# The largest-output pass without GpSimd's split, and masked attention with its bias row in two parts

## The chip, the cores and the metric

One core of one Trainium2 chip runs the kernel. The metric is the device time of one execution in microseconds (us); lower is better.

## The reference

A chain of four residual blocks on x of 16 x 256 x 512, with a context of the same shape, all in f32. `_layernorm` has no learned scale.

```
x = x + L0_xattn(layernorm(x), ctx)     # 16 heads of 64; two softmaxes: 77 text rows, 179 image rows
x = x + L0_ffn(layernorm(x))            # 1536 wide, quantized
x = x + L1_xattn(layernorm(x), ctx, ctx, mask)
x = x + L1_ffn(layernorm(x))            # two layers, 2048 wide, routed LoRA
```

In `L0_ffn` every activation is rounded to 16 bits with a scale from the largest magnitude of the whole tensor:

```
up, gate = act_qdq(x @ Wup.T), act_qdq(x @ Wgate.T)
gate = act_qdq(gate * fixed_qdq_u16(sigmoid(gate)))
o = act_qdq(gate * up);  return o @ Wdown.T
```

In `L1_xattn` queries and keys go through the same two linear maps: `p(t) = (t @ W1.T + b1) @ W2.T + b2`, `softmax(p(q) p(k)^T / sqrt(512) + mask) @ ctx`.

## The kernel before

The program is a row of phases, each with its own tiles (their names carry the phase) and a written order of instructions for each engine; engines meet through semaphores. PE is TensorE, DVE VectorE, ACT ScalarE, POOL GpSimd, SP SyncE, which issues most DMAs. An f32 product of full precision is made of three f32r matmuls over a high and a low part of each operand (`product`, L182; lines L186 to L188); the high part is a rounded copy, the low part the difference.

**The output maximum** (`output_maximum`, tiles `om`, L1430 to L1792) must know the largest magnitude of gate * up before the down projection can quantize it. It runs over 48 pieces n of 128 x 1024. For each, SP loads raw up values (L1509) and, every second piece, stored sigmoids (L1513); ACT scales them to int16 `up` (L1582) and writes the `gate` (L1584), and makes every other sigmoid itself (L1575), which DVE rounds into `sq` (L1647); DVE forms `outp` (L1664), the product `prod` of piece n+2 (L1657), and the piece's maximum (L1668). All of these are on one list for each engine, in the order of n.

Beside it the pass prepares the next attention. Both linear maps of query and key are folded into one 512 x 512 matrix (`gram`, n up to 15), and then the folded keys of the context are made in eight chunks of 512 rows, two context blocks x each. A block is loaded into the single buffer `cin` (L1518), turned by PE into PSUM `ctp` (`turn`, L1737), copied by ACT to `craw` (L1590), and POOL makes the high part (cast, L1697) and the low part (subtract, L1699) in `cT`. PE then makes four key groups `rb[i]` and one bias row `tb` of twelve matmuls each. `keys_due`, `bias_due` and `context_due` say at which piece each of these stands: keys (c, i) at n = 16 + 4c + i, contexts 2 to 15 at n = 15, 17, ... 41; contexts 0 and 1 are at n = 3 and 9. ACT adds the column to the keys (L1599) into one of two `rout` buffers, and SP stores them three pieces later (L1522), the bias rows too (L1527). After the last maximum POOL reduces over the partitions (L1727).

**The down projection** (`down`, tiles `dn`, L1795) follows; POOL only issues additions of finished rows to DRAM there.

**Masked attention** (`masked_attention`, tiles `ma`, L1915 to L2226) goes over 16 blocks b, staggered over steps s from FIRST = -3. DVE makes the statistics of x (L2045, L2050) and `var` (L2055); POOL raises it to the power -1/2 (L2016); DVE makes the shift, minus mean times that (L2061); ACT normalises (L2117); PE turns (L2179); ACT and DVE take the high and low part `xT` (L2124, L2065). Keys are split by ACT (L2130) and POOL (L2020), values by ACT (L2136) and POOL (L2024). PE starts each score tile with the bias row, a matmul of one row `trow` with `ones`, both f32 (L2189), then twelve matmuls of a product; DVE adds the mask and finds the maximum (L2073), ACT the exponentials (L2145), PE turns them and multiplies by the values. `LoraSides` (L2229) loads small matrices for the last phase in the meantime; its 20 loads are issued by POOL. `lora_ffn` (tiles `lf`) is not touched.

`wait_alone` (L108) puts a wait on an instruction of its own, with an increment of a spare semaphore behind it.

## Time and profile before

| | us |
|---|---|
| median of 3 runs | 3605.62 (3603.48 to 3608.56) |
| the profiled execution | 3610.11 |
| its span | 3608.4 |
| PE busy | 3250.0 (90%) |
| DVE busy | 1960.4 (54%) |
| ACT busy | 1554.8 (43%) |
| POOL busy | 841.9 (23%) |
| output pass, piece 0 to the last maximum | some 1961 to 2199 |
| masked attention | from some 2493 |

The four engines work beside each other, so shares do not add up. The mean granted clock of TensorE was 0.959 of full speed. Times of single instructions are us from the start of the span.

### The profile page before, as it was taken

How to read it: one execution, taken by the hardware profiler on the slowest of the kernel's cores; microseconds unless marked ns; L12 is line 12 of the kernel's file. 1: busy time of each engine (PE TensorE's matmuls, PEld its weight loads, DVE VectorE, ACT ScalarE, POOL GpSimd, SP SyncE). 2: the span in 40 equal slices, each digit the busy share in tenths (PEclk: the TensorE clock that was granted, in tenths of full speed). 3: DMA queues.
4: the chain of work that ended last, by engine and by line, in shares of the span. 5: the costliest groups of instructions: out<-in, count | busy, mean ns of one | idle time of the engine just before them, and what ended most of it. 6: DMA issues, size and time to landing. Idle time of an engine off the chain costs nothing. (4 is left out here: it accounts for less than half of the span.)

```text
span 3608.4 us, 51546 instructions
## 1 busy us (share of the span) xinstructions
PE 3250.0 (90%) x17336; PEld 2772.8 (77%) x17336; DVE 1960.4 (54%) x3277; ACT 1554.8 (43%) x2947; POOL 841.9 (23%) x1152
## 2 busy tenths in 40 slices
PE   7999979999999987998996886995968999999998
PEld 6989878888888875886885565884756777877776
DVE  3245467777777763555887996553863222222221
ACT  3222266666666652334776775553642111111110
POOL 0000066666666650000000440001730000000000
PEclk9999999999999998999998898997988999999999
DMA  6577654545455425554666676443642100111000
GB/s 182 146 242 229 206 166 145 149 137 150 135 146 152 135 82 198 185 188 150 225 217 218 193 244 214 164 167 112 219 140 79 50 21 21 36 35 36 30 24 12
DMA packets 362213, 503.42 MB, mean 140 GB/s; under 512 B 48835, under 2 KB 227379, under 8 KB 358081
## 3 DMA queue, kind: packets, MB, share of 16 engines
q1 hardware_dynamic: 359130, 491.16, 43.4%
q0 software_dynamic: 2864, 9.42, 0.7%
q8 instruction: 127, 2.08, 0.2%
q14 instruction: 92, 0.75, 0.1%
HBM read 292.83 MB, written 174.08 MB: 129 GB/s over the span
## 5 line engine op out<-in xcount | busy, mean ns | idle before, releaser
L2506 DVE SCALAR_TENSOR_TENSOR lf_hT<-lf_hb,lf_hT 128x512 fp32r<-128x512 f32 x128 | 88.6, 692 | 618.8 <-ACT lf_hT L2571 617.2
L2571 ACT ACTIVATE lf_hT<-lf_hb 128x512 fp32r<-128x512 f32 x128 | 76.6, 599 | 685.2 <-PE lf_py L188 636.3
L769 POOL TENSOR_TENSOR at_prob<-at_prob,at_rec 128x308 f32<-128x308 f32 (+1 forms) x256 | 261.7, 1045 | 264.0 <-DVE at_rec L811 263.4
L904 ACT ACTIVATE at_prob<-at_sc,at_nm 128x77 f32<-128x77 f32 (+1 forms) x1024 | 293.5, 383 | 41.4 <-DVE at_nm L798 41.4
L798 DVE TENSOR_REDUCE at_nm<-at_sc 128x4 f32<-128x308 f32 (+1 forms) x256 | 164.7, 685 | 171.4 <-PE at_sc L958 171.1
L917 ACT ACTIVATE at_pT<-at_tp 128x1024 fp32r<-128x1024 f32 x128 | 131.6, 1028 | 200.8 <-PE at_tp L968 200.8
L186 PE MATMUL lf_hb<-lf_xT,lf_w 128*128 128x512 f32 x512 | 204.9, 400 | 0.0
L188 PE MATMUL lf_hb<-lf_xT,lf_w 128*128 128x512 f32 x512 | 203.7, 398 | 0.0
L187 PE MATMUL lf_hb<-lf_xT,lf_w 128*128 128x512 f32 x512 | 203.2, 397 | 0.0
L188 PE MATMUL lf_py<-lf_w,lf_hT 128*128 128x512 f32 x512 | 202.6, 396 | 0.0
L186 PE MATMUL lf_py<-lf_w,lf_hT 128*128 128x512 f32 x512 | 202.5, 395 | 0.0
L187 PE MATMUL lf_py<-lf_w,lf_hT 128*128 128x512 f32 x512 | 202.0, 395 | 0.0
L186 PE MATMUL dn_py<-qf_wd,dn_om 128*128 128x512 f32 x384 | 150.8, 393 | 26.7 <-DVE dn_om L1868 26.7
L2446 POOL TENSOR_SCALAR lf_var<-lf_mv 128x1 f32<-128x1 f32 x32 | 7.2, 224 | 718.0 <-DVE lf_mv L2459 718.0
L804 DVE TENSOR_REDUCE at_sums<-at_prob 128x4 f32<-128x308 f32 (+1 forms) x256 | 172.8, 675 | 0.0
L186 PE MATMUL pg_bank<-pg_xs,qg_wg 128*128 128x512 f32 x384 | 153.4, 400 | 20.2 <-DVE pg_xs L1362 20.2
L756 POOL TENSOR_TENSOR at_ks<-at_kr,at_ks 128x512 fp32r<-128x512 f32 x128 | 164.8, 1287 | 14.6 <-ACT at_ks L911 14.6
L815 DVE TENSOR_TENSOR at_pT<-at_tp,at_pT 128x1024 fp32r<-128x1024 f32 x128 | 156.2, 1220 | 21.9 <-ACT at_pT L917 21.8
L186 PE MATMUL pu_bank<-pu_xs,qu_wu 128*128 128x512 f32 x384 | 150.6, 392 | 19.0 <-DVE pu_xs L1362 16.7
L186 PE MATMUL at_vq<-at_xT,xo_Wq 128*128 128x256 f32 x512 | 146.7, 287 | 17.6 <-DMA at_xT<-xn_parts 13.1
L186 PE MATMUL at_vq<-at_pT,at_vs 128*128 128x256 f32 x512 | 156.5, 306 | 0.9 <-DVE at_oT L821 0.8
L958 PE MATMUL at_sc<-at_ks,at_qs 128*128 128x256 f32 x1024 | 147.0, 287 | 7.1 <-DMA at_qs<-at_qst 7.1
(323 smaller groups left out, 9648.4 us busy)
## 6 DMA issues: line engine op xcount, KB each, us to landing
at_kr<-k_rows SPq DMA_DIRECT2D x256, 128.0 KB, 2.8
at_qs<-at_qst SPq DMA_DIRECT2D x512, 64.0 KB, 2.0
raw_gate<-pg_stage SPq DMA_DIRECT2D x96, 256.0 KB, 2.0
pu_rg<-raw_gate SPq DMA_DIRECT2D x96, 256.0 KB
raw_up<-pu_stage SPq DMA_DIRECT2D x96, 256.0 KB, 2.1
om_raw<-raw_up SPq DMA_DIRECT2D x48, 512.0 KB, 4.1
dn_raw<-raw_up SPq DMA_DIRECT2D x48, 512.0 KB, 3.8
xn_parts<-pr_xturned SPq DMA_DIRECT2D x32, 512.0 KB, 4.9
```

What stands on the lines that cost most here:

```text
L186: pe.matmul(out, lh, rh, start=start, stop=False, **kw)
L187: pe.matmul(out, lh, rl, start=False, stop=False, **kw)
L188: return pe.matmul(out, ll, rh, start=False, stop=stop, **kw)
L756: pool.tensor_tensor(ks[:, n % NK, :, 1, :], kr[:, n % NKR], ks[:, n % NK, :, 0, :].bitcast(F32), ALU.subtract).then_inc(k_low, 1)
L769: ins = pool.tensor_tensor(prob[:, i, :, lo:hi], prob[:, i, :, lo:hi], rec[:, z, g, :].unsqueeze(2).broadcast_to([P, 2 * NTE, hi - lo]), A ...
L798: ins = dve.tensor_reduce(nm[:, n % 2, g, :], sc[n % 2][:, :, lo:hi], AX_X, ALU.max, negate=True)
L804: dve.tensor_reduce(sums[:, z, g, :], prob[:, i, :, SEG[g][0]:SEG[g][1]], AX_X, ALU.add).then_inc(sum_done, 1)
L815: dve.tensor_tensor(pT[:, n % 2, 1], tp[:], pT[:, n % 2, 0].bitcast(F32), ALU.subtract).then_inc(pt_done, 1)
L904: ins = act.activation(prob[:, i, m, lo:hi], sc[n % 2][:, m, lo:hi], ACT.Exp, bias=nm[:, n % 2, g, m:m + 1])
L917: act.activation(pT[:, n % 2, 0], tp[:], ACT.Copy).then_inc(pt_hi, 1)
L958: ins = pe.matmul(sc[n % 2][:, h * NTE + m, :], qs[:, n % NQ, h, m * P:(m + 1) * P], ks[:, n % NK, h, part, :], start=part == 0, stop=part ...
L2506: dve.scalar_tensor_tensor(hT[:, i, 1, :], hb[i][:], 0.0, hT[:, i, 0, :].bitcast(F32), ALU.max, ALU.subtract).then_inc(h_done, 1)
```

## The change

In the output pass, ACT writes the high part of a context block straight from PSUM into `cT`, and DVE subtracts from the same PSUM tile to get the low part, one piece later, between `products` and `largest`. `craw`, POOL's casts and its subtracts are gone. Context loads are issued by POOL, key and bias stores by ACT one piece after the keys, and `rout` has four buffers with a semaphore each. The turn of a block waits for the low part of the block before. In the down projection POOL raises one column of ones to the power -1/2 at its start.

In masked attention the bias row is loaded as 16 x 256 (`traw`), split by ACT and DVE into two f32r parts, stored to DRAM and loaded as two rows (`trow`), and `ones` has two rows, so that the bias matmul is one f32r matmul. PE waits for it at block 0 only. DVE makes `minus` (minus the mean) before `var`, and POOL the shift, right behind the power. The 20 small loads are issued by SP.

The core of the diff:

```diff
@@ -1512,20 +1513,6 @@
 
-                def load_context(x):
-                    if x:
-                        sp.wait_ge(c_full, x)
-                    sp.dma_start(cin[:], ctx_in[x * S:(x + 1) * S, :].rearrange("(t p) d -> p t d", p=P)).then_inc(c_ready, 16)
-
-                def store_keys(c, i):
-                    sp.wait_ge(r_out, KD * c + i + 1)
-                    sp.dma_start(keys_d[NB * c:NB * (c + 1), :, i, :].rearrange("b p s -> p b s"), rout[:, i % 2, :].rearrange("p (b s) -> p b s", b=NB)
-                                 ).then_inc(r_stored[i % 2], 16)
-
-                def store_bias(c):
-                    sp.wait_ge(t_out, c + 1)
-                    sp.dma_start(bias_d[c:c + 1, :], trow[:, c % 2, :]).then_inc(t_stored[c % 2], 16)
...
-                        load_context(0)
...
-                    if n == 6:
-                        load_context(1)
-                    if context_due(n + 1):
-                        load_context(context_due(n + 1))
-                    if keys_due(n - 3):
-                        store_keys(*keys_due(n - 3))
-                    if bias_due(n - 3) is not None:
-                        store_bias(bias_due(n - 3))
                     if n == 24:
                         sp.wait_ge(gram_low, KD)
                         load_down((0,), (0, KD))
...
-                    if keys_due(n - 3):
-                        store_keys(*keys_due(n - 3))
-                    if n == N:
-                        sp.wait_ge(t_full, NCH - 1)
-                        load_down((0, 1), (2 * KD, 3 * KD))
-                    if bias_due(n - 3) is not None:
-                        store_bias(bias_due(n - 3))
+                sp.wait_ge(t_full, NCH - 1)
+                load_down((0, 1), (2 * KD, 3 * KD))
...
-                    sp.wait_ge(s, 16 * (KD // 2) * NCH)
+                    sp.wait_ge(s, 16 * NCH)
...
@@ -1584,25 +1556,37 @@
                 def context(x):
+                    c, lo = x // 2, x % 2 * S
                     act.wait_ge(c_full, x + 1)
-                    if x:
-                        act.wait_ge(c_low, x)
-                    act.activation(craw[:], ctp[:], ACT.Copy).then_inc(c_out, 1)
+                    if c >= 2:
+                        act.wait_ge(t_full, c - 1)
+                    if c == 1:
+                        act.wait_ge(gc_full, 1)
...
                     if c == 0 and i == 0:
                         act.wait_ge(gc_out, 2)
                         act.wait_ge(gb_low, 1)
-                    if KD * c + i >= 2:
-                        act.wait_ge(r_stored[i % 2], 16 * (2 * c + i // 2))
-                    act.activation(rout[:, i % 2, :], rb[i][:], ACT.Identity, bias=gcol[:, i:i + 1]).then_inc(r_out, 1)
...
 
                 def key_biases(c):
                     act.wait_ge(t_full, c + 1)
                     if c >= 2:
                         act.wait_ge(t_stored[c % 2], 16 * (c // 2))
                     act.activation(trow[:, c % 2, :], tb[0:1, :], ACT.Identity, bias=bb[0:1, 0:1]).then_inc(t_out, 1)
+
+                def store_keys(c, i):
+                    wait_alone(act, r_out, KD * c + i + 1, spacer)
+                    act.dma_start(keys_d[NB * c:NB * (c + 1), :, i, :].rearrange("b p s -> p b s"), rout[:, i, :].rearrange("p (b s) -> p b s", b=NB)
+                                  ).then_inc(r_stored[i], 16)
+
+                def store_bias(c):
+                    wait_alone(act, t_out, c + 1, spacer)
+                    act.dma_start(bias_d[c:c + 1, :], trow[:, c % 2, :]).then_inc(t_stored[c % 2], 16)
 
...
@@ -1630,13 +1614,19 @@
+                    if keys_due(n - 1):
+                        store_keys(*keys_due(n - 1))
+                    if bias_due(n - 1) is not None:
+                        store_bias(bias_due(n - 1))
                     if bias_due(n) is not None:
                         key_biases(bias_due(n))
                     if keys_due(n):
                         keys(*keys_due(n))
                     if context_due(n):
                         context(context_due(n))
+                store_keys(NCH - 1, KD - 1)
                 key_biases(NCH - 1)
+                store_bias(NCH - 1)
 
...
@@ -1656,6 +1646,11 @@
+                def context_low(x):
+                    c, lo = x // 2, x % 2 * S
+                    dve.wait_ge(c_hi, x + 1)
+                    dve.tensor_tensor(cT[c % 2][:, 1, :, lo:lo + S], ctp[:], cT[c % 2][:, 0, :, lo:lo + S].bitcast(F32), ALU.subtract).then_inc(c_low, 1)
...
@@ -1676,6 +1671,12 @@
                         products(n + 2)
+                    if n == 4:
+                        context_low(0)
+                    if n == 10:
+                        context_low(1)
+                    if context_due(n - 1):
+                        context_low(context_due(n - 1))
                     largest(n)
...
@@ -1687,28 +1688,22 @@
-                def context(x):
-                    c, lo = x // 2, x % 2 * S
-                    pool.wait_ge(c_out, x + 1)
-                    if c >= 2:
-                        pool.wait_ge(t_full, c - 1)
-                    if c == 1:
-                        pool.wait_ge(gc_full, 1)
-                    pool.tensor_copy(cT[c % 2][:, 0, :, lo:lo + S], craw[:]).then_inc(c_hi, 1)
-                    pool.wait_ge(c_hi, x + 1)
-                    pool.tensor_tensor(cT[c % 2][:, 1, :, lo:lo + S], craw[:], cT[c % 2][:, 0, :, lo:lo + S].bitcast(F32), ALU.subtract).then_inc(c_low, 1)
-
+                def load_context(x):
+                    if x:
+                        pool.wait_ge(c_full, x)
+                    pool.dma_start(cin[:], ctx_in[x * S:(x + 1) * S, :].rearrange("(t p) d -> p t d", p=P)).then_inc(c_ready, 16)
+
+                load_context(0)
                 pool.memset(betas, 1.0).then_inc(cleared, 1)
...
+                load_context(1)
...
                 for x in range(2, 2 * NCH):
-                    context(x)
...
@@ -1731,7 +1726,7 @@
                     if x:
-                        pe.wait_ge(c_out, x)
+                        pe.wait_ge(c_low, x)
...
@@ -1823,6 +1820,9 @@
+                pool.memset(one[:], 1.0).then_inc(one_made, 1)
+                pool.wait_ge(one_made, 1)
+                pool.tensor_tensor(one[:], one[:], neghalf[:, 0:1], ALU.pow).then_inc(one_raised, 1)
...
-        trow = ph.sb("trow", [1, B, S])
-        ones = ph.sb("ones", [1, P])
+        traw = ph.sb("traw", [B, S])
+        tsplit = ph.sb("tsplit", [B, 2, S], F32R)
+        trow = ph.sb("trow", [2, B, S], F32R)
+        ones = ph.sb("ones", [2, P], F32R)
...
@@ -1989,12 +1993,16 @@
-            sp.dma_start(trow[:].rearrange("o b s -> o (b s)"), bias_d.rearrange("c n -> (c n)").rearrange("(o n) -> o n", o=1)).then_inc(m_ready, 16)
+            sp.dma_start(traw[:], bias_d.rearrange("c (b s) -> (c b) s", b=NB)).then_inc(traw_ready, 16)
             load_keys(1)
...
+            sp.wait_ge(t_low, 1)
+            sp.dma_start(split_d, tsplit[:].bitcast(F32)).then_inc(t_stored, 16)
             load_keys(2)
             load_x(3)
...
+            sp.dma_start(trow[:].bitcast(F32), split_d.rearrange("b a s -> a b s")).then_inc(t_ready, 16)
             for s in range(LAST + 1):
...
@@ -2004,6 +2012,9 @@
                     load_x(s + 4)
+                for i in (2 * s - 6, 2 * s - 5):
+                    if 0 <= i < sides.LOADS:
+                        sides.load(sp, i)
...
@@ -2014,6 +2025,8 @@
                 pool.tensor_tensor(rstd[:, b % 2], var[:], neghalf[:, 0:NK], ALU.pow).then_inc(rstd_ready, 1)
+                pool.wait_ge(rstd_ready, b + 1)
+                pool.tensor_tensor(shift[:, b % 2], minus[:, b % 2], rstd[:, b % 2], ALU.mult).then_inc(shift_ready, 1)
...
 
-            pool.memset(ones[:], 1.0).then_inc(ones_made, 1)
...
                     dve.wait_ge(rstd_ready, b)
+                dve.tensor_scalar(minus[:, b % 2], mv[:, b % 2, :, 0], -1.0, None, ALU.mult)
                 dve.tensor_scalar(var[:], mv[:, b % 2, :, 1], EPS, None, ALU.add).then_inc(var_ready, 1)
-
-            def offset(b):
-                wait_alone(dve, rstd_ready, b + 1, spacer_d)
-                if b >= 2:
-                    dve.wait_ge(xn_ready, b - 1)
-                dve.scalar_tensor_tensor(shift[:, b % 2], mv[:, b % 2, :, 0], -1.0, rstd[:, b % 2], ALU.mult, ALU.mult).then_inc(shift_ready, 1)
...
@@ -2095,10 +2100,11 @@
                     turned_x(s + 1)
-                if 0 <= s + 2 < B:
-                    offset(s + 2)
                 if 0 <= s + 3 < B:
                     statistics(s + 3)
+                if s == FIRST:
+                    dve.wait_ge(t_high, 1)
+                    dve.tensor_tensor(tsplit[:, 1, :], traw[:], tsplit[:, 0, :].bitcast(F32), ALU.subtract).then_inc(t_low, 1)
...
@@ -2157,6 +2163,9 @@
                     keys_high(s + 2)
+                if s == FIRST + 1:
+                    act.wait_ge(traw_ready, 16)
+                    act.activation(tsplit[:, 0, :], traw[:], ACT.Copy).then_inc(t_high, 1)
...
@@ -2186,6 +2195,9 @@
                     cols = slice(t * P, (t + 1) * P)
+                    if b == 0 and t == 0:
+                        pe.wait_ge(ones_made, 1)
+                        pe.wait_ge(t_ready, 16)
                     pe.matmul(sc[b % 2][:, t, :], ones[:], trow[:, b, :], start=True, stop=False)
...
 
-            pe.wait_ge(ones_made, 1)
```

How the order of ACT's instructions changes in the output pass, at a pair of pieces with keys and a context. Before (`om_up`, `qf_gate` and `om_sig` belong to the pieces):

```order
L1584 ACTIVATE qf_gate<-om_prod,scal 128x1024
L1599 ACTIVATE om_rout<-om_rb,om_gcol 128x512
L1582 ACTIVATE om_up<-om_raw,scal 128x1024
L1584 ACTIVATE qf_gate<-om_prod,scal 128x1024
L1575 ACTIVATE om_sig<-qf_gate,scal 128x1024
L1599 ACTIVATE om_rout<-om_rb,om_gcol 128x512
L1590 ACTIVATE om_craw<-om_ctp 128x1024
L1582 ACTIVATE om_up<-om_raw,scal 128x1024
```

and after:

```order
L1556 ACTIVATE qf_gate<-om_prod,scal 128x1024
L1574 ACTIVATE om_rout<-om_rb,om_gcol 128x512
L1554 ACTIVATE om_up<-om_raw,scal 128x1024
L1556 ACTIVATE qf_gate<-om_prod,scal 128x1024
L1547 ACTIVATE om_sig<-qf_gate,scal 128x1024
L1584 DMA folded_keys<-om_rout 128x2x256
L1574 ACTIVATE om_rout<-om_rb,om_gcol 128x512
L1565 ACTIVATE qf_wd<-om_ctp 128x4x256
L1554 ACTIVATE om_up<-om_raw,scal 128x1024
L1556 ACTIVATE qf_gate<-om_prod,scal 128x1024
```

Each key store now stands on ACT, one piece behind its activation, and the context goes to `qf_wd`, where `cT` lies.

The end of POOL's down projection and the start of its masked attention, in order. Before, at the first power (the row `ISA` is an instruction that loads code for POOL):

```order
L2026 MEMSET ma_ones 1x128
L2016 ISA
L2016 TENSOR_TENSOR ma_rstd<-ma_var,neghalf 128x2
L2020 TENSOR_TENSOR ma_rT<-ma_rraw,ma_rT 128x1024
L2016 TENSOR_TENSOR ma_rstd<-ma_var,neghalf 128x2
```

and after, where the down projection starts (the first three rows) and where masked attention does:

```order
L1823 MEMSET dn_one 128x1
L1825 ISA
L1825 TENSOR_TENSOR dn_one<-dn_one,neghalf 128x1
...
L2039 MEMSET ma_ones 2x128
L2027 TENSOR_TENSOR ma_rstd<-ma_var,neghalf 128x2
L2029 TENSOR_TENSOR ma_shift<-ma_minus,ma_rstd 128x2
L2033 TENSOR_TENSOR ma_rT<-ma_rraw,ma_rT 128x1024
```

The `ISA` row of the power's line has moved to the start of the down projection, and the shift follows each power on POOL.

## Rows read from the trace of the kernel before

**Rows 1.** Windows: stretch, us, busy PE, PEld, DVE, ACT, POOL, clock, DMA share, GB/s.

```profile
1976.30:2047.70 71.40, 54.37 (x207) 34.88 (x208) 70.33 (x57) 53.58 (x60) 28.71 (x19) 0.81 0.58 178
2047.70:2197.10 149.40, 123.67 (x531) 98.44 (x529) 139.37 (x107) 114.37 (x126) 55.22 (x26) 0.91 0.76 240
2493.00:2502.00 9.00, 0.00 (x0) 0.00 (x0) 1.71 (x5) 1.06 (x1) 0.00 (x0) 0.50 0.90 320
2560.80:2637.90 77.10, 77.10 (x467) 63.15 (x466) 72.59 (x136) 53.97 (x90) 57.66 (x42) 1.00 0.76 245
```

**Rows 2.** Groups by line, 1960 to 2201 us: busy, mean ns, idle before.

```profile
L1657 DVE TENSOR_TENSOR om_prod<-qf_gate,om_sq 128x1024 f32<-128x1024 int16 x48 | 81.7, 1702 | 18.1 <-DMA om_sq<-gate_sigmoids 17.9
...
L1699 POOL TENSOR_TENSOR qf_wd<-om_craw,qf_wd 128x1024 fp32r<-128x1024 f32 x16 | 48.3, 3021 | 10.1 <-issue 8.9
```

**Rows 3.** Timeline of DVE, output pass: start us, duration us, line, instruction.

```profile
2047.75 1.21 DVE L1664 TENSOR_TENSOR om_outp<-qf_gate,om_up 128x1024 f32<-128x1024 int16 x1
...
2183.26 1.23 DVE L1664 TENSOR_TENSOR om_outp<-qf_gate,om_up 128x1024 f32<-128x1024 int16 x1
...
2190.88 1.23 DVE L1664 TENSOR_TENSOR om_outp<-qf_gate,om_up 128x1024 f32<-128x1024 int16 x1
```

**Rows 4.** Timeline of POOL and DVE in the output pass.

```profile
2163.79 3.25 POOL L1699 TENSOR_TENSOR qf_wd<-om_craw,qf_wd 128x1024 fp32r<-128x1024 f32 x1
...
2164.71 3.41 DVE L1657 TENSOR_TENSOR om_prod<-qf_gate,om_sq 128x1024 f32<-128x1024 int16 x1
```

**Rows 5.** Timeline of all engines, start of masked attention.

```profile
2495.45 0.40 SPq L1992 DMA_DIRECT2D ma_trow<-key_biases  x1
...
2498.67 0.17 DVE L2055 TENSOR_SCALAR ma_var<-ma_mv 128x2 f32<-128x2 f32 x1
2510.04 0.73 POOL L2016 TENSOR_TENSOR ma_rstd<-ma_var,neghalf 128x2 f32<-128x2 f32 x1 [17.05 <-issue]
...
2510.92 2.18 DVE L2061 SCALAR_TENSOR_TENSOR ma_shift<-ma_mv,ma_rstd 128x2 f32<-128x2 f32 x1 [12.09 <-POOL ma_rstd L2016]
...
2524.87 1.22 PE L2189 MATMUL ma_sc<-ma_trow,ma_ones 1*128 1x256 f32 x2
```

**Rows 6.** Costliest groups of the page.

```profile
L815 DVE TENSOR_TENSOR at_pT<-at_tp,at_pT 128x1024 fp32r<-128x1024 f32 x128 | 156.2, 1220 | 21.9 <-ACT at_pT L917 21.8
```

**Rows 7.** Timeline of SP's DMA queue in the output pass.

```profile
2164.04 0.44 SPq L1522 DMA_DIRECT2D folded_keys<-om_rout  x1
```

**Rows 8.** DMA issues, 1961 to 2201 us: KB each, median us to landing.

```profile
om_cin<-in_ctx_dram SPq DMA_DIRECT2D x16, 512.0 KB, 5.3
```

**Rows 9.** Timeline of PE in masked attention.

```profile
2599.97 0.69 PE L2189 MATMUL ma_sc<-ma_trow,ma_ones 1*128 1x256 f32 x2
...
2600.81 0.28 PE L187 MATMUL ma_sc<-ma_rT,ma_xT 128*128 128x256 f32 x1
2600.93 0.27 PE L188 MATMUL ma_sc<-ma_rT,ma_xT 128*128 128x256 f32 x1
...
2608.57 0.69 PE L2189 MATMUL ma_sc<-ma_trow,ma_ones 1*128 1x256 f32 x2
...
2651.61 0.69 PE L2189 MATMUL ma_sc<-ma_trow,ma_ones 1*128 1x256 f32 x2
...
2659.34 0.69 PE L2189 MATMUL ma_sc<-ma_trow,ma_ones 1*128 1x256 f32 x2
```

**Rows 10.** Timeline of DVE and POOL in masked attention.

```profile
2531.15 4.05 DVE L2055 TENSOR_SCALAR ma_var<-ma_mv 128x2 f32<-128x2 f32 x1
...
2602.12 2.38 POOL L2020 TENSOR_TENSOR ma_rT<-ma_rraw,ma_rT 128x1024 fp32r<-128x1024 f32 x1 [2.11 <-ACT ma_rT L2130]
2604.46 2.40 POOL L2024 TENSOR_TENSOR ma_val<-ma_cin,ma_val 128x1024 fp32r<-128x1024 f32 x1
...
2602.27 2.25 DVE L2061 SCALAR_TENSOR_TENSOR ma_shift<-ma_mv,ma_rstd 128x2 f32<-128x2 f32 x1
...
2606.25 0.64 DVE L2055 TENSOR_SCALAR ma_var<-ma_mv 128x2 f32<-128x2 f32 x1
```

More of the change, by code:

```diff
@@ L1930, in masked_attention @@
         rstd = ph.sb("rstd", [P, 2, NK])
+        minus = ph.sb("minus", [P, 2, NK])
         shift = ph.sb("shift", [P, 2, NK])
@@ L2035, in _ @@
                     sides.clear(pool)
-                for i in range(2 * s - 2, 2 * s):
-                    if 0 <= i < sides.LOADS:
-                        sides.load(pool, i)
         @block.vector
@@ L2258, with load @@
     LOADS = 2 * (1 + E) + 2 * 5
-    def load(self, pool, i):
+    def load(self, sp, i):
         layer, i = i % 2, i // 2
```

49 lines of the change are left out of this document (28 added, 21 removed).

## The prediction

> **What bounds the kernel now.** I read the windows view first, for the engines' busy time in four stretches that the change touches [rows 1]. In the output-maximum pass (`om`), pieces 0 to 15 take 71.40 us with VectorE (DVE) busy for 70.33 of them, and pieces 16 to 47, beside which the eight key chunks run, 149.40 us with DVE busy for 139.37, ScalarE (ACT) for 114.37 and TensorE (PE) for 123.67 at a granted clock of 0.91. DVE is what ends last. In the steady steps of masked attention (`ma`) PE is busy for 77.10 of 77.10 us. The fourth stretch, 2493 to 2502, has no matmul at all: it is the start of `ma`.
>
> Second, the groups by line say why DVE is so busy: `prod` has a mean of 1702 ns over 48, and GpSimd's (POOL's) subtract at L1699 of 3021 ns over 16 [rows 2]. Third, DVE's timeline: a pair of pieces without POOL beside it, from `outp` at 2183.26 to `outp` at 2190.88, takes 7.62 us; but 27 pieces lie between the `outp` of piece 16 (2047.75) and of piece 43 (2183.26), so 135.5/13.5 = 10.04 us for a pair [rows 3]. In the difference stands the POOL pair: `prod` is issued at 2164.71 while the subtract runs (2163.79 for 3.25 us) and takes 3.41 us instead of 1.22 [rows 4]. It ends 1.08 us after the subtract, that is, it did not begin before POOL had ended.
>
> Fourth, the start of `ma` [rows 5]: `var` is there at 2498.84, the power that needs it runs at 2510.04, with "17.05 <-issue" of idle before it on POOL: nothing that the profile shows was waited for. The shift, issued when the power is done, is held by POOL's first subtract and ends at 2513.10. ACT's first normalisation and all of PE stand behind it.
>
> **The change, part by part.**
>
> *Output pass, pieces 16 to 47.* Out go POOL's 16 casts and 16 subtracts, and with them what DVE lost to them. In comes a DVE subtract per context, from PSUM and one SBUF tile, 128x1024. No such instruction runs in this pass; the nearest row is attention's L815, the same form and size, mean 1220 [rows 6]. So DVE needs 7.62 + 1.2 = 8.8 us for a pair. ACT needs its busy time of now, 114.37/149.40 x 10.04 = 7.69 us, and now issues two key stores and, every second pair, a bias store. Such a store takes SP's queue 0.44 us [rows 7]; its price on ACT no row shows. With SP's, ACT comes to 7.69 + 2 x 0.44 + 0.1 = 8.7 us; from below it costs nothing (7.7), from above twice the row (9.6), should ACT drain before an issue and fill again behind it. PE needs 123.67/149.40 x 10.04 = 8.3 us. Three engines within 0.5 us that wait for each other don't run at the longest one's own time: I take 9.05, between DVE's 8.8 and ACT's upper 9.6 and nearer DVE's, since that one rests on rows of DVE itself. Gain: 13.5 x (10.04 - 9.05) = **13.4 us** (ends: 13.5 x 0.44 = 6 with ACT at 9.6; 13.5 x 1.24 = 17 with DVE at 8.8).
>
> *Pieces 0 to 15.* Three contexts lie here. Each lost DVE some 2.2 us on one operation (3.41 - 1.22 [rows 4]) and now costs 1.2; the second also about 0.8 by its cast. Gain 3 x 1.0 + 0.8 = **3.8 us** (ends 0 and 6).
>
> *Queues.* SP loses 56 issues, which hid behind its wait for ACT; nothing. Context loads now sit on POOL's queue, which has nothing else left to do but the fold; they wait for the turn before, as on SP. There is one `cin` buffer: issue and landing must fit between one turn and the next. A pair of 9.05 less a turn of about 1.0 less some 0.8 of issue leaves 7.2 us, the median load took 5.3 [rows 8]. Nothing, if POOL's loads land like SP's. The four key buffers free ACT's keys from the store before; ACT was not last, so nothing more. The store one piece later has a full chunk before its buffer comes round. At the pass's end the last piece's maximum still decides; `key_biases` and its store end in the next few us, as today.
>
> *Down projection.* One memset and one power on a single column on POOL, which waits for its first result there: nothing. It makes the code load fall here: the order of instructions has POOL's "ISA" row (the load) now in front of this power, and none left in `ma`.
>
> *Start of `ma`.* With the code there, power (0.73 [rows 5]) and shift follow `var`: 2498.84 + 0.73 + about 0.7 = 2500.3, against 2513.10. But ACT now waits for `traw` ahead of its first normalisation. That load is issued where `trow` is now, 2495.45, behind 2.25 MB; at 320 GB/s [rows 1] those take 7.0 us from 2493, so it lands at 2500 to 2503 (my estimate from these rows); with ACT's copy, 2502.2. Gain **10.9 us** (ends 7, if it lands at 2506, and 12.8). DVE waits in the same place, with the statistics of block 1 behind it, which are wanted 8 us later. PE's new wait for `trow`: split store issued at 2502.7, landing and load 4 us each behind 1 MB of keys and x, so 2511; PE would want it at 2524.87 - 10.9 - 1.6 = 2512.4. Nothing, narrowly; up to 3 us if late.
>
> The Trainium skill ("GPSIMD Engine Reference", section Instruction dispatch) says that the first call of a freshly loaded kernel waits about 6 us for its code, with no instruction in the profile. The row has the same shape but 11.2 us; by the page's figure the term would be some 6 and the sum -31.
>
> *Ramp of `ma`.* Up to block 3 the chain runs through the shift that is held by POOL's subtract, 1.6 us per block: two blocks, **3.3 us** (ends 0 and 5). PE's bias product: f32 pairs of 0.62 us each at full clock (two of its four records: 0.69 [rows 9]) become one f32r pass, 2600.81 to 2600.93, 0.12 [rows 9]: 2 x 0.5 = 1.0 us per block. It counts where PE is last: one block at half clock, where the pair is 1.22 [rows 5] in place of some 0.25, two of them **2.0 us**, and the last blocks, 2651.61 to 2659.34 = 7.73 us each [rows 9], two and a half of them, **2.5 us** (ends for both 2 and 6).
>
> *Steady steps.* PE's 8.60 us (2599.97 to 2608.57 [rows 9]) would become 7.6. But the next limit is there already [rows 10]: POOL's two subtracts, 2602.12 to 2606.86, begin when ACT has cast the keys, and DVE's `var` (issued 2606.25, usually 0.17) ends only at 2606.89; behind it logits, exponentials, ACT's next `xT`. Without the held shift DVE comes to `minus` and `var` at 2604.1, inside the first subtract. If they are let in only when both are over, `var` ends at 2606.95 and the loop remains 8.6 to 8.7: **+0.5 us** over ten steps. For this speaks the `var` at 2531.15, which took 4.05 us, over the end of a subtract and four memsets, back to back [rows 10]. ACT no longer waits for the shift; it waits for the maximum instead.
>
> Side loads go from POOL to SP (about 0.5 us each, two a step); SP has time.
>
> Sum: 13.4 + 3.8 + 10.9 + 3.3 + 2.0 + 2.5 - 0.5 = 35.4 us off. Against the profiled execution's 3610.11 that is 3574.7; the median of the runs shown is 4.5 us lower, 3605.62, so I say **3570 us**.
>
> **Rivals.**
>
> *A, the lock opens between two subtracts.* At 2604.46 the held shift did get in, between POOL's first and second subtract (it ended 2604.52) [rows 10]. If the two `tensor_scalar` do too, `var` is there 2.2 us sooner and the steps fall to PE's 7.6: ten more us, 3560. For it: that row. Against: the row at 2531.15, and that these two are another kind of operation.
>
> *B, the output pass is bound by ACT.* An issue on ACT costs 0.9 us or so and the pair stays at 9.6 to 9.8: 3 to 6 us instead of 13.4, 3579 (3575 to 3584). For it: ACT's 8.7 is already 0.1 under DVE's. Against: SP's 0.44.
>
> *C, slower: the context loads come late.* If POOL's loads land more than 7.2 us after issue, PE's turn waits, the chunk slips, and the waits of ACT and DVE in order of program pass it to every piece. Each us beyond costs 14; the gains of 35 are eaten at 7.2 + 2.5 = 9.7 us, and at 10.5 it would be 3617. Against: POOL has nothing to compute then. Chance 0.04.
>
> The Trainium skill ("SBUF — State Buffer", section Who interferes with whom) has descriptors of a POOL-issued DMA starve while DVE is in its two-port modes; no run so far shows such a load. By it the load would wait for the `tensor_scalar` that each pair has, which is no more than 0.7 us, and C would still need another 2.
>
> *D, the early power doesn't keep the code.* The load returns before `ma`; the 10.9 go, 3581. Against: no other POOL code is called between, by the order of instructions.
>
> **How the numbers follow.** Forecast 0.54, A 0.18, B 0.18, D 0.06, C 0.04. The low end is A with the output term at its upper end (3560 - 4, less a little for the ramp's: 3554); the high end is B or D with traw late or the ramp term missing (3581 + 4, and up to 7 for both together: 3592). A run tells apart about 0.2%, 7 us. Faster by more: all but C and the tail of B and D together, 0.93; within: 0.03; slower: 0.04.
>
> **What would show it.** In `om`: `prod` with a mean near 1.22 us, the new subtract at 1.2, pairs of 9.0 us; POOL without busy time there; ACT's gap behind an issue 0.4 (right) or 0.9 (B); PE waiting for `om_cin` (C). In `ma`: the power within 1 us of `var`, ACT's first normalisation at 10 to 11 us earlier against `var`, its release the `traw` load; bias rows of PE at 0.12; steady period 8.6 with `var` ending where POOL's second subtract does (right) or 7.6 (A). It is wrong if the pair is over 9.6 or under 8.7, or if the first normalisation still stands 14 us behind `var`.

## The result, and the profile after

| | before | changed |
|---|---|---|
| median, us | 3606.10 (4 runs, 3603.48 to 3608.56) | 3578.22 (4 runs, 3576.30 to 3586.45) |
| ratio | | 0.992, 95% interval 0.9905 to 0.9935 |
| profiled execution, us | 3610.11 | 3577.34 |
| span, us | 3608.4 | 3575.7 |
| POOL busy, us | 841.9 | 777.6 |

The kernel became faster by 27.9 us. Forecast were 35 (3570), range 3554 to 3592. The sum came out well by luck: two of its parts were wrong in opposite ways. The output pass gave less than said, masked attention more.

The windows view of the changed kernel, core 0; the stretches are pieces 0 to 15, pieces 16 to 47, and steady masked attention:

```profile
core 0: us, PE busy (x) PEld busy (x) DVE busy (x) ACT busy (x) POOL busy (x), PEclk, DMA share, GB/s
1978.70:2047.00 68.30, 47.45 (x160) 28.84 (x161) 66.02 (x59) 50.74 (x57) 18.45 (x15) 0.73 0.55 167
2047.00:2195.10 148.10, 129.47 (x577) 103.77 (x575) 132.21 (x122) 116.38 (x129) 8.69 (x12) 0.95 0.79 255
2532.00:2619.50 87.50, 87.50 (x550) 75.03 (x550) 63.62 (x160) 65.84 (x110) 60.93 (x42) 1.00 0.81 252
```

Against [rows 1], pieces 0 to 15 went from 71.4 to 68.3 us, the rest from 149.4 only to 148.1, though POOL, which held DVE up before, is busy for 8.69 us instead of 55.22. DVE is busy for 132.21 us of it now and waits for the rest. Pair for pair, from the `outp` of piece 16 (2047.01) to that of piece 43 (2179.90): 132.9/13.5 = 9.84 us, where [rows 3] gave 10.04.

DVE's groups in the output pass, in the view of [rows 2] (busy, mean ns, idle before):

```profile
L1647 DVE TENSOR_TENSOR om_prod<-qf_gate,om_sq 128x1024 f32<-128x1024 int16 x48 | 60.4, 1259 | 23.0 <-DMA om_sq<-gate_sigmoids 23.0
L1652 DVE TENSOR_TENSOR qf_wd<-om_ctp,qf_wd 128x1024 fp32r<-128x1024 f32 x16 | 19.5, 1216 | 0.0
```

`prod` fell from 1702 to 1259 ns, and the new subtract takes 1216. So DVE's `prod` no longer stands behind a subtract of POOL's, and the new instruction costs what was said. But DVE waits now. The view of waits, 2050 to 2180 us (in total, times, longest), for the change:

```profile
ACT qf_wd L1565 <- PE om_ctp L1732: 21.2, 11, 3.6
PE om_ctp L1732 <- DVE qf_wd L1652: 15.8, 8, 4.0
DVE om_prod L1647 <- DMA om_sq<-gate_sigmoids: 13.4, 8, 3.3
```

and for before:

```profile
DVE om_prod L1657 <- DMA om_sq<-gate_sigmoids: 7.6, 4, 2.9
```

In before the view has no wait of ACT for a turn. ACT waited 16.9 us there, nine times, for the key stores that read its two `rout` buffers; with four buffers the change has none of that.

One round of this in the timeline of the changed kernel, which is to be read downwards as a chain:

```profile
2099.80 1.22 DVE L1652 TENSOR_TENSOR qf_wd<-om_ctp,qf_wd 128x1024 fp32r<-128x1024 f32 x1
...
2103.16 1.03 PE L1732 MATMUL om_ctp<-ident,om_cin 128*128 128x128 f32 x8
...
2104.23 1.03 ACT L1565 ACTIVATE qf_wd<-om_ctp 128x1024 fp32r<-128x1024 f32 x1 [2.04 <-PE om_ctp L1732]
2104.42 0.37 ACTq L1584 DMA_DIRECT2D folded_keys<-om_rout  x1
2105.15 1.14 ACT L1554 ACTIVATE om_up<-om_raw,scal 128x1024 int16<-128x1024 f32 x1
...
2106.32 3.54 SPq L1510 DMA_DIRECT2D om_raw<-raw_up  x2
...
2108.37 1.13 ACT L1554 ACTIVATE om_up<-om_raw,scal 128x1024 int16<-128x1024 f32 x1
...
2109.90 0.44 SPq L1514 DMA_DIRECT2D om_sq<-gate_sigmoids  x1
...
2115.08 1.23 DVE L1647 TENSOR_TENSOR om_prod<-qf_gate,om_sq 128x1024 f32<-128x1024 int16 x1 [0.82 <-DMA om_sq<-gate_sigmoids]
```

DVE's low part ends at 2101.02; until then PE may not turn the next block into the one `ctp`. In this round the bias row's matmuls on PE end later still, and it is they that hold the turn to 2103.16; over the 130 us, the waits above give PE 15.8 us for the low part. ACT comes to the context early, waits 2.04 us for the turn, and all its later work is late with it: `up` at 2105.15, the next one at 2108.37. SP's raw loads wait for them (the two issues last from 2106.32 to 2109.86, as the second waits for the second `up`, done at 2109.50), the sigmoid load stands behind them in SP's queue (2109.90), and DVE waits for it till 2115.08. The row 2104.42 is a key store issued on ACT: it lies within the context's copy, and from that copy to the next activation it is 0.92 us.

The start of masked attention, to be set against [rows 5]:

```profile
2495.19 0.16 DVE L2066 TENSOR_SCALAR ma_var<-ma_mv 128x2 f32<-128x2 f32 x1
2495.54 0.73 POOL L2027 TENSOR_TENSOR ma_rstd<-ma_var,neghalf 128x2 f32<-128x2 f32 x1 [6.06 <-DVE ma_var L2066]
2496.35 0.20 POOL L2029 TENSOR_TENSOR ma_shift<-ma_minus,ma_rstd 128x2 f32<-128x2 f32 x1
...
2498.34 0.42 ACT L2168 ACTIVATE ma_tsplit<-ma_traw 16x256 fp32r<-16x256 f32 x1 [2.72 <-DMA ma_traw<-key_biases]
2498.66 1.50 ACT L2123 ACTIVATE ma_xn<-ma_y,ma_shift,ma_rstd 128x512 f32<-128x512 f32 x2
```

The power starts 0.35 us after `var` does (11.37 before), and the shift takes 0.20 behind it. The first normalisation is at 3.5 us behind `var` (14.6 before). What it waits for is `traw`, as predicted, landed at 2498.34, 6.4 us after its issue at 2491.95.

A steady step, against [rows 9, 10]:

```profile
2589.83 2.40 POOL L2033 TENSOR_TENSOR ma_rT<-ma_rraw,ma_rT 128x1024 fp32r<-128x1024 f32 x1 [2.27 <-ACT ma_rT L2136]
2592.19 2.41 POOL L2037 TENSOR_TENSOR ma_val<-ma_cin,ma_val 128x1024 fp32r<-128x1024 f32 x1
...
2591.80 0.46 DVE L2065 TENSOR_SCALAR ma_minus<-ma_mv 128x2 f32<-128x2 f32 x1
2592.17 0.16 DVE L2066 TENSOR_SCALAR ma_var<-ma_mv 128x2 f32<-128x2 f32 x1
...
2595.64 0.38 PE L2201 MATMUL ma_sc<-ma_trow,ma_ones 2*128 2x256 f32 x1
2595.95 0.39 PE L187 MATMUL ma_sc<-ma_rT,ma_xT 128*128 128x256 f32 x1
...
2595.75 1.03 ACT L2130 ACTIVATE ma_xT<-ma_xtp 128x1024 fp32r<-128x1024 f32 x1 [1.61 <-PE ma_xtp L2188]
...
2603.72 1.03 ACT L2130 ACTIVATE ma_xT<-ma_xtp 128x1024 fp32r<-128x1024 f32 x1 [1.61 <-PE ma_xtp L2188]
```

The period is 7.97 us (8.60 before), and PE is busy for 87.50 of 87.50 us. `minus` was issued at 2591.80, inside POOL's first subtract, and ended at 2592.26, when that one was over and POOL's second one had begun. The bias row takes 0.31 us from its start to the next matmul, not 0.12. By the windows above TensorE's granted clock in these steps is 1.00, its upper level (2.4 GHz), as in [rows 1].

### Where the time went

The profiled executions differ ahead of the output pass by several us where the instructions are the same: its first `outp` is at 1976.31 in before, at 1978.73 in the change, and between 1969.85 and 1983.48 in the kernels below. So the table has the time from the first `outp` of the pass to the end of the span (**the rest**). It is 1632.1 us before (one trace) and 1597.0 in the change, 35.1 less; a second trace of the change gave 1596.9. The medians, which contain what lies ahead, moved by 27.9; no row of the changed code accounts for the other 7 us. Two traces of the changed kernel itself differ by 4.8 us ahead of the pass. The gain of the whole kernel is the 27.9.

| stretch | before | changed | difference | forecast |
|---|---|---|---|---|
| pieces 0 to 15 (1976.31 to 2047.75; 1978.73 to 2047.01) | 71.4 | 68.3 | -3.2 | -3.8 |
| pieces 16 to 43 (to 2183.26; 2179.90) | 135.5 | 132.9 | -2.6 | -13.4 |
| from there to `var` of block 0 (2498.67; 2495.19) | 315.4 | 315.3 | -0.1 | 0 |
| `var` of block 0 to its first normalisation | 14.6 | 3.5 | -11.1 | -10.9 |
| `xT` of block 0 to block 4 (2516.87 to 2557.02; 2502.22 to 2532.01) | 40.2 | 29.8 | -10.4 | -5.3 |
| `xT` of block 4 to block 15 (to 2651.71; 2619.65) | 94.7 | 87.6 | -7.1 | +0.5 |
| behind it | 956.7 | 956.1 | -0.6 | -2.5 |

From the first normalisation to the first `xT` both kernels take 3.6 us. How far traces of the same code differ can be read from the kernels below: pieces 16 to 43 took 134.3 to 135.5 us in the three traces with the old output pass, and 132.3 to 133.0 in five with that of the change (the change, c0, b1, b2, b3; a2 is an exception). So the 2.6 us are 1.2 to 3.2, whichever traces are paired, and far from 13.4 in any case.

### The profile page after: what moved, and what is told of

Same layout as the page of the kernel before. It is cut to its first block and busy times, and to the rows that moved or that the text cites. A ratio compares the mean times of both kernels' runs of the same rounds, so it can differ in the third digit from the quotient of the medians.

```text
span 3575.7 us, 51505 instructions
## 1 busy us (share of the span) xinstructions
PE 3239.0 (91%) x17304; PEld 2769.6 (77%) x17304; DVE 1912.3 (53%) x3294; ACT 1553.6 (43%) x2948; POOL 777.6 (22%) x1136
## 5 line engine op out<-in xcount | busy, mean ns | idle before, releaser
L187 PE MATMUL pg_bank<-pg_xs,qg_wg 128*128 128x512 f32 x384 | 153.5, 400 | 20.4 <-DVE pg_xs L1363 20.4
L187 PE MATMUL at_vq<-at_xT,xo_Wq 128*128 128x256 f32 x512 | 147.2, 288 | 19.7 <-DMA at_xT<-xn_parts 12.7
```

The source lines that it names most:

```text
L187: pe.matmul(out, lh, rh, start=start, stop=False, **kw)
```

## The experiments

Medians are set against those of before that were measured beside them, and the rest against the 1597.0 of the change or the 1632.1 of before.

| kernel | median | before there | ratio, 95% | rest | a pair, pieces 16 to 43 |
|---|---|---|---|---|---|
| the change again (c0) | 3577.76 | 3606.70 | 0.991 (0.9895 to 0.9925) | 1596.9 | 9.85 |
| a1 masked attention and power only | 3582.96 | 3609.12 | 0.9929 (0.9907 to 0.9951) | 1601.2 | 10.01 |
| a2 output pass only | 3603.70 | 3609.12 | 0.9982 (0.9971 to 0.9992) | 1622.8 | 9.63 |
| a5 low part early | 3568.09 | 3609.12 | 0.9886 (0.9864 to 0.9907) | 1585.2 | 8.96 |
| a4 sigmoid load first | 3562.72 | 3609.12 | 0.987 (0.9847 to 0.9893) | 1584.3 | 8.90 |
| b4 both | 3558.80 | 3608.12 | 0.9865 (0.9848 to 0.9881) | 1583.5 | 8.92 |
| b1 no early power | 3584.28 | 3608.12 | 0.993 (0.9914 to 0.9947) | 1607.2 | 9.85 |
| b2 bias row in f32 | 3585.23 | 3608.12 | 0.9935 (0.9918 to 0.9953) | 1604.0 | 9.82 |
| b3 shift on DVE | 3589.67 | 3608.12 | 0.9949 (0.9931 to 0.9967) | 1608.1 | 9.80 |
| a3 early power only | 3597.23 | 3606.70 | 0.9969 (0.9955 to 0.9982) | 1621.3 | 9.95 |
| c1 stores on SP | 3583.14 | 3606.70 | 0.9925 (0.9908 to 0.9941) | 1602.5 | 9.99 |
| c2 context loads on SP | 3643.48 | 3606.70 | 1.0099 (1.0083 to 1.0115) | 1665.8 | 14.67 |

c0 is the changed kernel itself, with no edit, measured beside a3, c1 and c2:

> The changed kernel once more, beside the three below on the same chip, as their reference. 26 to 30 us under before.

28.9 us under before, its rest within 0.1 us of the first trace's.

### The two halves apart (a1, a2)

a1 is the changed kernel with the function `output_maximum` of before, of which this is the heart:

```diff
-                    act.activation(cT[c % 2][:, 0, :, lo:lo + S], ctp[:], ACT.Copy).then_inc(c_hi, 1)
+                    act.activation(craw[:], ctp[:], ACT.Copy).then_inc(c_out, 1)
...
-                        pe.wait_ge(c_low, x)
+                        pe.wait_ge(c_out, x)
```

Expected:

> The changed kernel with the output pass of before, so only the early power and the new masked attention are in. Theory 1 (from the two traces: the pass gave 3.5 us, masked attention 29): 29 us under before, about 3577. Rival (the prediction's split: pass 17, attention 18): 18 under before, about 3588.

26.2 us under before, and the rest 30.9 less. The prediction's 18 for this half is out.

a2 is before with the changed `output_maximum`:

```diff
-                    act.activation(craw[:], ctp[:], ACT.Copy).then_inc(c_out, 1)
+                    act.activation(cT[c % 2][:, 0, :, lo:lo + S], ctp[:], ACT.Copy).then_inc(c_hi, 1)
...
-                        pe.wait_ge(c_out, x)
+                        pe.wait_ge(c_low, x)
```

Expected:

> Before with only the output pass of the change. Theory 1: 3 to 4 us under before, 3602.5, which a timing cannot tell from nothing; DVE waits some 13 us for its sigmoid loads, ACT some 20 us for PE's turn. Rival (the pass is worth 17, and masked attention paid it back): 3589.

5.4 us under before, the rest 9.3 less, of which 5.5 in pieces 16 to 43. That is more than the 3.5 read from the two traces, though nearer to it than to 17, and its 130.0 us there stand outside the 132.3 to 133.0 of the same pass in the other traces. The halves add up to 31.6 by medians (27.9 together) and to 40.2 by the rest (35.1 together): the pass alone was somewhat quicker ahead of the old masked attention, with DVE's wait for the sigmoids at 10.0 us instead of 13.4. Why it was is open.

### The ring through `ctp` (a5, a4, b4)

a5 moves DVE's low part ahead of the piece's output:

```diff
                     if n % 2 == 0 and n + 2 < N:
                         rounded(n + 2)
+                    if n == 4:
+                        context_low(0)
+                    if n == 10:
+                        context_low(1)
+                    if context_due(n - 1):
+                        context_low(context_due(n - 1))
                     outputs(n)
                     if n + 2 < N:
                         products(n + 2)
```

Its six lines behind `products` are gone. Expected:

> The changed kernel with DVE's low part of a context placed ahead of the piece's output, two operations (2.3 us) earlier; everything else is as in the change. Theory ring (PE's turn waits for the low part, ACT for the turn, the scaled up values and with them SP's loads are late, and DVE waits for the sigmoids): ACT's wait for the turn falls from 21 us to under 6, DVE's wait for the sigmoids from 13 to under 4, the pair falls from 9.84 towards 8.9, 10 to 12 us under the change, about 3567. Rival memory (the loads are late because the DMA traffic of a faster pass is too dense): ACT's wait goes, the sigmoid wait stays, the time stays within 3 us of the change.

Waits of a5, 2050 to 2180 us:

```profile
ACT qf_wd L1565 <- PE om_ctp L1732: 8.3, 11, 1.3
DVE om_prod L1647 <- DMA om_sq<-gate_sigmoids: 3.1, 2, 2.4
```

ACT's wait for the turn fell from 21.2 to 8.3 us, DVE's for the sigmoids from 13.4 to 3.1, the pair to 8.96 us, the rest by 11.8. The theory said all four, though it had ACT's wait under 6. The rival "the memory is too dense" is out: the same bytes in less time, and the wait went.

a4 leaves the low part where the change has it, and cuts the chain at SP:

```diff
                 def load_main(n):
-                    if n >= 2:
-                        sp.wait_ge(up_ready, n - 1)
-                    sp.dma_start(raw[...]).then_inc(raw_ready[n % 2], 16)
                     if n % 2:
                         if n >= 2:
                             sp.wait_ge(prod_done, n - 1)
                         sp.dma_start(sq[:, 1, :], ...).then_inc(sq_ready, 16)
+                    if n >= 2:
+                        sp.wait_ge(up_ready, n - 1)
+                    sp.dma_start(raw[...]).then_inc(raw_ready[n % 2], 16)
```

> The changed kernel with SP issuing the sigmoid load of an odd piece ahead of that piece's raw load (it stands behind it in the change, and so behind the wait for ACT's up values). Theory ring: DVE's wait for the sigmoids falls from 13 us to under 6, ACT's wait for the turn stays, 5 to 9 us under the change, about 3571. Rival memory: the wait stays at 10 or more and the time within 3 us of the change.

```profile
ACT qf_wd L1565 <- PE om_ctp L1732: 15.1, 13, 2.0
DVE om_prod L1647 <- DMA om_sq<-gate_sigmoids: 1.5, 1, 1.5
```

ACT still waits for the turn (15.1 us, 6 less than in the change), but DVE for the sigmoids only 1.5, and the pair is 8.90 us. So the wait for the turn costs by what stands behind it: with the sigmoid load in time, DVE has next to no gap. The gain, 12.7 us of the rest, is over the 5 to 9 expected.

b4 has both edits:

> The changed kernel with both edits of the output pass: the sigmoid load ahead of the raw load, and DVE's low part ahead of the output. Theory ring: the two cut the same ring at two places, so they don't add up (15 and 10 us alone): DVE is then busy all the time at 8.8 us a pair, 16 to 19 us under the change. Rival (two separate losses): 23 or more.

13.5 us of the rest, the pair at 8.92: hardly more than either alone (12.7 and 11.8), since DVE's own 8.8 is nearly reached; DVE is busy for 130.35 of 135.60 us. The median is 49.3 us under the before measured beside it, where c0 was 28.9 under its own, so 20.4 by the medians. The 16 to 19 expected lie between the two; that the pair is no shorter than in a4 speaks against two separate losses. It is the lowest median tried, 0.9865 (0.9848 to 0.9881), but neither a4 nor a5 can be told from it by the intervals.

### The queues (c1, c2)

c1 gives the key and bias stores back to SP, in the places of before, with the four buffers kept:

```diff
-                    wait_alone(act, r_out, KD * c + i + 1, spacer)
-                    act.dma_start(keys_d[...], rout[:, i, :]...).then_inc(r_stored[i], 16)
+                    sp.wait_ge(r_out, KD * c + i + 1)
+                    sp.dma_start(keys_d[...], rout[:, i, :]...).then_inc(r_stored[i], 16)
```

> The changed kernel with key and bias stores issued by SP three pieces after the keys, as before, four buffers kept. Theory from the trace (an issue on ACT lies within its activations and costs it nothing, 1.04 us from start to start across one; on SP it stands in the queue of the sigmoid loads that DVE waits for): 0 to 4 us over the change, DVE's wait for the sigmoids from 13 to 13 to 18 us. The prediction's term (0.44 us of ACT for each issue, 1 us a pair): ACT gains 13 us and the pass up to that, 3 or more under the change.

Waits of c1, 2050 to 2170 us:

```profile
ACT qf_wd L1584 <- PE om_ctp L1736: 24.8, 11, 3.1
DVE om_prod L1651 <- DMA om_sq<-gate_sigmoids: 14.8, 10, 2.6
```

and two rows of its ACT:

```profile
2103.48 1.03 ACT L1584 ACTIVATE qf_wd<-om_ctp 128x1024 fp32r<-128x1024 f32 x1 [2.04 <-PE om_ctp L1736]
2104.40 1.14 ACT L1573 ACTIVATE om_up<-om_raw,scal 128x1024 int16<-128x1024 f32 x1
```

5.4 us over c0 by the medians, a little over the 0 to 4 expected and with intervals that overlap; 5.5 by the rest, the pair 9.99. From the context's copy to the next activation it is 0.92 us, with no issue between, exactly as in the change with one. So the prediction's 0.44 us of ACT for each issue is out: it is nothing. DVE waits for sigmoids 14.8 us in a stretch of 120 where the change has 12.1. That this is what the move to ACT was worth fits, but is not shown alone: the stores also went back from one piece behind the keys to three.

c2 gives the context loads back to SP, where before has them:

```diff
+                    if context_due(n + 1):
+                        load_context(context_due(n + 1))
```

on SP (with contexts 0 and 1 at n = 0 and 6), and none on POOL. Expected:

> The changed kernel with the context loads issued by SP where before has them. Theory: SP waits for PE's turn with the raw and sigmoid loads behind it, and that turn is now late because of the low part; DVE's wait for the sigmoids rises, 3 to 10 us over the change. Rival C (a load issued by POOL comes later than one of SP's): the turn comes sooner and the time is 2 or more under the change.

66 us over c0, and slower than before. The direction was expected, the size was not. Waits, 2050 to 2170 us:

```profile
DVE om_prod L1657 <- DMA om_sq<-gate_sigmoids: 52.6, 8, 8.8
...
PE om_ctp L1733 <- DVE qf_wd L1662: 44.5, 8, 8.7
...
SPq L1519 <- PE om_ctp L1733: 103.2, 8, 14.6
```

and SP's queue in the timeline:

```profile
2108.54 0.38 SPq L1519 DMA_DIRECT2D om_cin<-in_ctx_dram  x1
2108.96 0.47 SPq L1510 DMA_DIRECT2D om_raw<-raw_up  x1
2109.47 0.68 SPq L1514 DMA_DIRECT2D om_sq<-gate_sigmoids  x1
...
2123.57 0.38 SPq L1519 DMA_DIRECT2D om_cin<-in_ctx_dram  x1
```

SP waits 103 of 120 us for the turn, because its load may only go once `cin` is read; raw and sigmoid loads stand behind it. The turn waits for the low part, the low part stands on DVE behind a `prod` that waits for just those sigmoids (issued at 2109.47, `prod` at 2115.10, the low part at 2120.24). The ring is closed through the lists of three engines, SP, DVE and PE, and one round of it, 15.03 us from 2108.54 to 2123.57, is a pair. In before the same load was at the same place on SP, but the turn waited for ACT's copy only. So of the edits in the pass one (the turn that waits for the low part) needs another (the load off SP's list).

### Masked attention, part by part (b1, a3, b2, b3)

b1 is the change without the memset and the power in `down`:

```diff
-                pool.memset(one[:], 1.0).then_inc(one_made, 1)
-                pool.wait_ge(one_made, 1)
-                pool.tensor_tensor(one[:], one[:], neghalf[:, 0:1], ALU.pow).then_inc(one_raised, 1)
```

> The changed kernel without the one-column power at the start of the down projection. Theory (the early power is what moves the code load): the 11 us between var and the first power of masked attention are back, less the wait for the bias row that now lies beside them (the first normalisation of the change begins 3.5 us behind var): 8 to 9 us over the change, so about 17 under before. Rival (the load is cheap here, or hidden by the wait for the bias row): within 3 us of the change.

```profile
2501.92 0.16 DVE L2061 TENSOR_SCALAR ma_var<-ma_mv 128x2 f32<-128x2 f32 x1
...
2512.78 0.73 POOL L2022 TENSOR_TENSOR ma_rstd<-ma_var,neghalf 128x2 f32<-128x2 f32 x1 [16.69 <-issue]
...
2513.91 1.52 ACT L2118 ACTIVATE ma_xn<-ma_y,ma_shift,ma_rstd 128x512 f32<-128x512 f32 x2 [7.81 <-POOL ma_shift L2024]
```

The load is back in its old place: 10.86 us from `var` to the power, with nothing waited for. The first normalisation stands 12.0 us behind `var`, 8.5 more than in the change, as expected. The rest is 10.2 us longer; the median is 23.8 us under the before beside it, where c0 is 28.9 under, so the medians give 5.1 (ratios 0.993 and 0.991, with intervals that overlap), and not the 8 to 9 expected.

a3 is before with these three lines and nothing else:

```diff
+                pool.memset(one[:], 1.0).then_inc(one_made, 1)
+                pool.wait_ge(one_made, 1)
+                pool.tensor_tensor(one[:], one[:], neghalf[:, 0:1], ALU.pow).then_inc(one_raised, 1)
```

> Before with nothing but the one-column power at the start of the down projection. Theory: the first power of masked attention follows var within 0.5 us instead of 11.2, the shift is then held 2.3 us by POOL's first subtract, and everything behind it comes 10 to 11 us sooner; steady period 8.6 as before: 10 us under before. Rival (the first blocks wait for their loads anyway, which are issued at the same time as before): under 5 us.

```profile
2498.93 0.73 POOL L2021 TENSOR_TENSOR ma_rstd<-ma_var,neghalf 128x2 f32<-128x2 f32 x1 [6.04 <-DVE ma_var L2060]
2499.82 2.17 DVE L2066 SCALAR_TENSOR_TENSOR ma_shift<-ma_mv,ma_rstd 128x2 f32<-128x2 f32 x1 [1.07 <-POOL ma_rstd L2021]
...
2502.12 1.52 ACT L2122 ACTIVATE ma_xn<-ma_y,ma_shift,ma_rstd 128x512 f32<-128x512 f32 x2 [3.03 <-DVE ma_shift L2066]
```

9.5 us under before, 10.8 by the rest. The power follows `var` by 0.35 us, and the shift on DVE is held by POOL's first subtract for 2.17 us, as the prediction said of before. So two instructions on one column are a third of the whole change. Rival D is out by this and by b1.

b2 has the bias row as one f32 row again, loaded straight from `key_biases`, without the split and its waits:

```diff
-        trow = ph.sb("trow", [2, B, S], F32R)
-        ones = ph.sb("ones", [2, P], F32R)
+        trow = ph.sb("trow", [1, B, S])
+        ones = ph.sb("ones", [1, P])
```

> The changed kernel with the bias row as before: one f32 row, an f32 matmul, no split, no round trip through DRAM. Theory (the steps are PE's, and the f32r row takes 0.64 us off each): the steady period is 8.6 us again, 10 steps x 0.64 and some 3 us of the ramp back, less 2 us at the start where ACT waits for the row: 6 to 8 us over the change. Rival (the steps were set by the ring through the shift and POOL's subtracts, and it is the shift on POOL that opened them): period 8.0, within 3 us.

```profile
2560.00:2620.00 60.00, 60.00 (x364) 49.20 (x363) 44.13 (x105) 41.20 (x71) 38.97 (x29) 1.00 0.81 250
```

PE is busy for all 60 us again, and the period is 8.61 us. The rest is 7.0 us longer, within the 6 to 8 expected.

b3 has the shift on DVE, behind `turned_x`, and no `minus`:

```diff
-                pool.tensor_tensor(shift[:, b % 2], minus[:, b % 2], rstd[:, b % 2], ALU.mult)...
+                dve.scalar_tensor_tensor(shift[:, b % 2], mv[:, b % 2, :, 0], -1.0, rstd[:, b % 2], ALU.mult, ALU.mult)...
```

> The changed kernel with the shift made by DVE behind the power as before, and no minus. Theory (two limits stood at the same height, PE's 8.6 and the ring through the shift that POOL's subtract holds): the period stays at 8.5 to 8.6 though PE has 0.64 us less to do, PE shows gaps, 6 to 10 us over the change. Rival (PE alone set it): period 8.0, and only the ramp's 3 us come back.

```profile
2546.10:2622.80 76.70, 74.31 (x458) 61.61 (x457) 73.21 (x136) 53.26 (x93) 48.91 (x27) 1.00 0.83 246
```

```profile
2590.91 2.27 DVE L2068 SCALAR_TENSOR_TENSOR ma_shift<-ma_mv,ma_rstd 128x2 f32<-128x2 f32 x1
...
2594.92 0.61 DVE L2062 TENSOR_SCALAR ma_var<-ma_mv 128x2 f32<-128x2 f32 x1
...
2590.76 2.40 POOL L2030 TENSOR_TENSOR ma_rT<-ma_rraw,ma_rT 128x1024 fp32r<-128x1024 f32 x1 [2.87 <-ACT ma_rT L2140]
2593.12 2.38 POOL L2034 TENSOR_TENSOR ma_val<-ma_cin,ma_val 128x1024 fp32r<-128x1024 f32 x1
```

and of the waits, 2546.1 to 2622.8 us:

```profile
ACT ma_xn L2127 <- DVE ma_shift L2068: 15.0, 9, 1.7
```

The period is 8.52 us (nine steps, 2546.15 to 2622.79), and PE now has gaps: 74.31 of 76.70. The shift is held through POOL's first subtract, ACT's normalisation waits for it in each of the nine steps, and `var`, issued at 2594.92, is held through the end of the second (2595.50). The rest is 11.1 us longer, just over the 6 to 10 expected. So there were two limits, PE at 8.60 and the ring through the shift at 8.52, and either edit alone gives 0.1 us at most of the 0.64 that both give.

## Why the prediction was right in sum and wrong in parts

- **Pieces 16 on: wrong (13.4 forecast, 2.6 came to piece 43).** The gain is under the lower end of 6 us, and the pair, at 9.84, was over the 9.6 that the prediction itself gave as a sign of being wrong. DVE's own 8.8 us a pair was right; a4, b4 and a5 run at 8.90 to 8.96. The step that failed is the one that costs the queues: "they wait for the turn before, as on SP. [...] Nothing". The changed wait of the turn, `c_low` for `c_out`, was named nowhere in the sum. It puts DVE's low part and a turn between ACT's two contexts, and what stands behind ACT's wait (`up`, then SP's raw load, then the sigmoid load) is what DVE waits for. Taking 9.05 because "Three engines within 0.5 us that wait for each other don't run at the longest one's own time" was a margin of 0.25 us in place of a chain that the code shows; it was 1.04.
- **ACT's issue: wrong.** 0.44 us each were forecast; with and without an issue it is 0.92 us from the context's copy to the next activation. Rival B came near the outcome for the pass (9.6 to 9.8, where 9.84 came), with the wrong cause.
- **Pieces 0 to 15: right** (3.8 forecast, 3.2 came).
- **Context loads on POOL: right as far as it went.** They landed in 5.1 us at the median (5.3 on SP), so rival C did not come, neither did the starving of descriptors of which the Trainium skill speaks ("SBUF — State Buffer", section Who interferes with whom) at a size that shows here. But the step saw only a risk in the move; c2 shows 66 us in its favour, as long as the turn waits for the low part.
- **The early power and the start: right** (10.9 forecast, 11.1 came; `traw` released the first normalisation, at 6.4 us after its issue). The price of the load is the row's 11, not the 6 of the Trainium skill's "GPSIMD Engine Reference", section Instruction dispatch.
- **Ramp: half right.** The shift's 1.6 us per block was there (8.11 to 6.38 us from block 0 to 1, and 8.11 again in b3), but the sum for blocks 0 to 4 was 10.4 us, not 5.3. Between blocks 1 and 2 4.1 us went, where before had `var` held for 4.05 us (2531.15 [rows 10]) by POOL's subtract and memsets; in the change that block's `var` is done at 2513.12, before they begin at 2515.32. With the shift back on DVE (b3) `var` is held for 4.03 us there and the 11.3 us from block 1 to 2 are back. Between 3 and 4 another 4.2 went (12.3 to 8.2 us), where PE's mean granted clock was 0.65 before and 0.89 in the change, by the windows view of the two stretches. PE is busy throughout in both, and the other kernels line up: 9.8 us at 0.78 in a1, 8.8 at 0.87 in b3, 7.9 at 1.00 in b2. The masked attention of a1 is that of the change, so 1.7 of the 4.2 us come with the clock and not with an edit of this phase. The prediction had 2.0 us there, for the bias rows at half clock.
- **Steady steps: wrong, rival A had the mechanism** (its period of 7.6 was too low by what the bias row cost more; 7.97 came). The claim that failed is "if they are let in only when both are over". The two `tensor_scalar` are let in when POOL's first subtract ends (2592.26 against 2592.23), so `var` (2592.33) is done 2.3 us before the second one ends. The row at 2531.15, on which the claim rested, shows a `var` issued within the second subtract with memsets right behind it, and here the same kind of instruction is issued within the first one. What tells the two cases apart is open: no run had memsets behind a first subtract.
- **The bias row: mis-sized.** 1.0 us a step was forecast from 0.12 per pass, 0.64 came: the pass over two rows costs 0.31 to the next matmul, half of the f32 pair's 0.62, where a product's matmuls, 128 rows each, follow each other by 0.12. There are two such rows in a block, so 0.62 us. And behind the last `xT` 0.6 us came, not 2.5, since only one block's bias rows lie there; what the blocks before it gained is in the steady steps.

## What to carry to other kernels

When a change makes a buffer come free later (here a PSUM tile that is read twice), follow the new wait through every queue until it comes back to the engine that you want to relieve; the sum of that engine's own work is only the floor. Where two engines meet a limit within 0.1 us of each other, one edit alone shows next to nothing (0.1 us of 0.64 here), so it has to be tried with the other before it is dropped. And the list of DMAs that one engine issues in order is part of such a ring: moving the sigmoid load by one place gave as much as moving the arithmetic.

## What the runs showed of the hardware

- A DMA issued by ACT costs its activations nothing here: 0.92 us from the context's copy to the next activation with an issue of 0.37 us within it, and the same 0.92 in c1 without one.
- The code load for POOL's power stands between `var` and the power at the start of masked attention: 11.37 us from start to start in before, 10.86 in b1, and 0.35 in the change. At the start of the down projection POOL is idle ahead of the power for 8.88 us in the change and 8.98 in c0, and for 8.3 to 12.0 in the other kernels that have it there; the stretch up to `var` is no longer for it (315.3 us against 315.4).
- The granted clock of PE over pieces 16 to 47 was 0.91 before (PE busy for 123.67 of 149.40 us), 0.95 in the change (129.47 of 148.10), 0.98 in b4 (123.78 of 135.60) and 0.80 in c2 (144.70 of 215.50).
